# Second expert layer wholly in high and low parts, with the expert blocks' work on the other engines put in another order

## The reference, cut to what matters

```
z      = layer_norm(x)                      # 4096 tokens x 256
assign = argmax(z @ centroids.T)            # one of 8 experts for each token
xn     = layer_norm(z) * ln_g[e] + ln_b[e]
h      = relu(xn @ w1[e].T + b1[e])         # first layer:  256 -> 1024
y      = z + h @ w2[e].T + b2[e]            # second layer: 1024 -> 256
out    = x + sigmoid(z . centroid[e]) * y + (1 - sigmoid(..)) * z
```

## Time and profile before

| what | value |
|---|---|
| time, median of 3 runs | 1053.16 us (1052.61 to 1053.6) |
| the profiled execution's own time | 1052.73 us |
| its span | 1050.9 us |
| PE busy | 1041.6 us (99%) |
| DVE, ACT, POOL busy | 844.9, 688.7, 565.3 us |
| expert blocks on TensorE | from about 799.6 us to the end |

### The profile page before, as it was taken

One profiled execution on the slowest core, in us unless ns is written; L12 is line 12 of the kernel. 1 busy time (PEld: TensorE's weight loads), 2 busy tenths in 40 slices (PEclk: granted clock), 3 DMA queues, 4 the chain that ended last, 5 costly groups with the idle time before them and its releaser, 6 DMA issues.

```text
span 1050.9 us, 24670 instructions
## 1 busy us (share of the span) xinstructions
PE 1041.6 (99%) x8610; PEld 940.5 (89%) x8610; DVE 844.9 (80%) x1979; ACT 688.7 (66%) x1838; POOL 565.3 (54%) x665
## 2 busy tenths in 40 slices
PE   9999999999999999999999999999999999999997
PEld 7889898988888888889898989889888999999997
DVE  7878888878888888888888879888887797767663
ACT  6765757675666767666757575766566666676761
POOL 1744464646454555545464646465444667566663
PEclk9999999999999999999999999999999999999999
DMA  6665657585757576767667585856356868777760
GB/s 212 160 169 148 170 156 189 146 215 142 201 146 197 142 193 155 200 156 197 159 168 185 142 210 137 213 144 171 91 153 196 307 198 294 250 234 234 249 194 31
DMA packets 159666, 190.57 MB, mean 181 GB/s; under 512 B 17454, under 2 KB 149038, under 8 KB 154673
## 3 DMA queue, kind: packets, MB, share of 16 engines
q1 hardware_dynamic: 155088, 179.09, 62.4%
q0 software_dynamic: 3360, 8.53, 2.2%
q10 hardware_dynamic: 1088, 1.31, 0.4%
HBM read 65.72 MB, written 46.07 MB: 106 GB/s over the span
## 4 chain that ended last, share of the span: by engine, by line
PE 96%; DVE 2%; POOL 1%; ACT 1%; DMA 0%; issue 0%; POOLq 0%; DVEq 0%
PE psum L742 17%; PE psum L775 16%; PE psum L812 11%; PE psum L902 10%; PE psum L791 10%; PE psum L827 9%; PE psum L761 8%; PE psum L938 6%; PE psum L932 5%; PE psum L830 1%; PE psum L883 1%; PE psum L914 1%; DVE neg_max L1410 1%; DMA c_in<-in_ctx_in 0%; PE psum L856 0%; DVE w_lo L1545 0%
## 5 line engine op out<-in xcount | busy, mean ns | idle before, releaser
L1823 POOL TENSOR_TENSOR prob<-prob,inv_sum 128x512 f32<-128x512 f32 x172 | 177.7, 1047 | 190.1 <-DVE inv_sum L1416 189.2
L1133 ACT ACTIVATE prob<-psum,neg_max 128x256 f32<-128x256 f32 x344 | 160.2, 478 | 38.8 <-DVE neg_max L1410 38.5
L1410 DVE TENSOR_REDUCE neg_max<-psum 128x2 f32<-128x512 f32 x256 | 161.9, 672 | 27.7 <-PE psum L791 27.5
L1422 DVE STREAM_TRANSPOSE prob<-prob 128x512 f32<-128x512 f32 x172 | 118.5, 698 | 12.3 <-POOL prob L1823 11.9
L1823 POOL TENSOR_TENSOR w_ring<-w_ring,inv_sum 128x512 f32<-128x512 f32 x76 | 78.1, 1041 | 76.0 <-DVE inv_sum L1416 75.7
L1140 ACT ACTIVATE head_out_hi<-psum 128x512 fp32r<-128x512 f32 x52 | 31.1, 597 | 105.6 <-PE psum L812 102.4
L1119 ACT ACTIVATE v_n<-psum 128x512 f32<-128x512 f32 x128 | 77.9, 608 | 26.7 <-PE psum L775 22.7
L1108 ACT ACTIVATE k_hi<-psum 128x512 fp32r<-128x512 f32 x128 | 77.0, 603 | 22.0 <-PE psum L742 21.3
L1461 DVE TENSOR_TENSOR k_lo<-psum,k_hi 128x512 fp32r<-128x512 f32 x128 | 85.7, 674 | 0.0
L742 PE MATMUL psum<-kv_t_hi,w_hi 128*128 128x512 f32 x252 | 85.0, 419 | 0.0
L775 PE MATMUL psum<-w_hi,kv_t_hi 128*128 128x512 f32 x256 | 80.2, 395 | 0.4 <-DVE k_lo L1461 0.4
(11 more groups left out here) (215 smaller groups left out, 2952.4 us busy)
## 6 DMA issues: line engine op xcount, KB each, us to landing
sorted_rows<-filler SPq DMA_DIRECT2D x54, 660.0 KB
prob_t<-prob SPq DMA_DIRECT2D x172, 128.0 KB, 2.8
w_ring<-prob SPq DMA_DIRECT2D x172, 128.0 KB, 2.7
w<-in_experts SPq DMA_DIRECT2D x19, 1024.0 KB, 7.8
w_ring<-in_experts SPq DMA_DIRECT2D x18, 1024.0 KB, 6.7
prob_t<-w_ring SPq DMA_DIRECT2D x76, 128.0 KB, 2.8
w_ring<-w_ring SPq DMA_DIRECT2D x76, 128.0 KB, 2.7
w_ring<-normed SPq DMA_DIRECT2D x56, 128.0 KB, 3.0
```

The source lines that it names most:

```text
L1133: act.activation(prob_at(u, bb)[:, :, parity, i], scores_i, ACT.Exp, bias=neg_max[:, at, i:i + 1], accum_out=prob_sum[:, at, i:i + 1]).the ...
L1410: dve.tensor_reduce(neg_max[:, (4 * u + n) % 8, :], psum[:, n, :].rearrange("p (i j) -> p i j", i=2), AXIS_X, ALU.max, negate=True).then_i ...
L1422: dve.transpose(probs, probs).then_inc(s_quad, 1)
L1823: pool.tensor_tensor(probs, probs, inverse, ALU.mult).then_inc(s_soft, 1)
```

## The change

The second layer of the blocks from slot 1 on is made wholly in parts: all four hidden pieces are split, all 2048 elements of the second weights are split, and the float32 products are gone. The hidden pieces pass through two places (`hid_raw[:, piece % 2]`), so relu of a piece waits for the split of the piece two before. Products of the low weights come last of the three passes, with the wait for them just ahead. On ScalarE and VectorE the first weights are split three blocks ahead instead of two, `high_weights_2` stays last on ScalarE, and VectorE does `low_weights_1` between the two halves of `finish`. The second weights' buffer is free again when its low part is made, not when the products have run.

```
 def load_weights_2(s):
-    if s >= NW2:
-        wait_made(sp, ("fy", s - NW2, 1))
+    if s == NW2:
+        wait_made(sp, ("fy", 0, 1))
+    elif s > NW2:
+        sp.wait_ge(f_w2l, s - NW2 - FIRST_SPLIT + 1)

 def layer_2_split(s):                                   # TensorE
+    pe.wait_ge(f_w2h, s - FIRST_SPLIT + 1)
+    pe.wait_ge(f_hl, FC // 2 * (s - FIRST_SPLIT + 1))
+    def products(bank, i, n): ...                       # 8 products of pass n
     for i in range(2):
         bank = begin(("fy", s, i))[:, 0:d_model]
-        # in_parts: 3 passes x 4; plain: 4 float32 products
+        products(bank, i, 0)
+        products(bank, i, 1)
+        if i == 0:
+            pe.wait_ge(f_w2l, s - FIRST_SPLIT + 1)
+        products(bank, i, 2).then_inc(f_y, 1)

 def relu_parts(s):                                      # ScalarE
     for i in range(FC // 2):
         act.wait_ge(f_h, FC // 2 * (s - 1) + i + 1)
-        if i < FS // 2 and s > FIRST_SPLIT:
-            act.wait_ge(f_hl, FS // 2 * (s - 1 - FIRST_SPLIT) + i + 1)
-        elif i == FS // 2 and s >= 2:
-            wait_made(act, ("fy", s - 2, 1))
+        piece = FC // 2 * (s - FIRST_SPLIT) + i
+        if piece >= 2:
+            act.wait_ge(f_hl, piece - 1)

 # ScalarE, loop
-for s in range(n_early, n_slots):
-    run(s + 2, (normalise_rows,), (high_weights_1,))
+for s in range(n_early - 1, n_slots):
     run(s + 1, (relu_parts,))
     run(s + 2, (row_gain_bias,))
+    run(s + 3, (normalise_rows,), (high_weights_1,))
     run(s + 1, (high_weights_2,))

 # VectorE: ahead of late_blocks and in the loop
+low_weights_1(5)
 late_blocks()
 finish(2)
-for s in range(n_early, n_slots):
-    run(s + 2, (low_weights_1,))
+for s in range(n_early - 1, n_slots):
     run(s + 1, (split_hidden,))                         # 4 pieces, was 2
     run(s + 2, (split_xn,))
     run(s + 3, (transpose_rows,))
-    run(s, (finish,))
+    run(s, (finish_half, 0))
+    run(s + 3, (low_weights_1,))
+    run(s, (finish_half, 1))

 def high_weights_2(s), low_weights_2(s):                # ScalarE, GpSimd
-    w2_ring[s % NW2][:, 0:FS * d_model]                 # 1024 elements
+    w2_ring[s % NW2][:]                                 # 2048 elements
```

More of the change, by code:

```diff
@@ L320, in build @@
             hid_raw = y_t[:].rearrange("p c b t -> p c (b t)")
[L321 to L322 removed]
+            w2_hl = [[w[:].rearrange(rule)[:, 0:n_w].rearrange("p (f d) -> p f d", f=FC) for w in pair] for pair, rule in
                      ((head_out, "p b c t -> p (b c t)"), (w_o, "p c n -> p (c n)"))]
@@ L919, in layer_2_split @@
                 def layer_2_split(s):
[L921 to L933, removed]
-                        return last
@@ L936, in plain @@
[L936 to L943, removed]
@@ L955, in layer_2_split, with products @@
-                    bank = begin(("fy", s, 1))[:, 0:d_model]
-                    plain(bank, 1, True)
-                    in_parts(bank, 1, False).then_inc(f_y, 1)
+                    pe.wait_ge(f_w2h, s - FIRST_SPLIT + 1)
+                    pe.wait_ge(f_hl, FC // 2 * (s - FIRST_SPLIT + 1))
+                    def products(bank, i, n):
+                        hw, hx = PASSES[n]
+                        for f in range(FC):
+                            last = pe.matmul(bank, hid_hl[hx][:, s % 2, f, i * P:(i + 1) * P], w2_hl[s % 2][hw][:, f, :],
+                                             start=(n == 0 and f == 0), stop=(n == 2 and f == FC - 1))
+                        return last
@@ new lines, in layer_2_split @@
+                    if s == FIRST_SPLIT:
+                        banks = [begin(("fy", s, i))[:, 0:d_model] for i in range(2)]
+                        for i in range(2):
+                            products(banks[i], i, 0)
+                            products(banks[i], i, 1)
+                        pe.wait_ge(f_w2l, 1)
+                        for i in range(2):
+                            products(banks[i], i, 2).then_inc(f_y, 1)
+                        return
+                    for i in range(2):
+                        bank = begin(("fy", s, i))[:, 0:d_model]
+                        products(bank, i, 0)
[3 more added lines that the diff above has]
+                        products(bank, i, 2).then_inc(f_y, 1)
@@ L1636, in low_weights_1, with split_hidden @@
                                       ALU.subtract).then_inc(f_wl, 1)
-                def split_hidden(s):
-                    for i in range(FS // 2):
+                def split_hidden(s, pieces=range(FC // 2)):
+                    for i in pieces:
                         dve.wait_ge(f_ha, FC // 2 * (s - 1) + i + 1)
@@ new lines, in split_hidden, with finish_half @@
+                        raw = hid_raw[:, (FC // 2 * (s - FIRST_SPLIT) + i) % 2, :]
+                        then_next(dve.tensor_copy(hi, raw))
+                        dve.tensor_tensor(lo, raw, hi, ALU.subtract).then_inc(f_hl, 1)
+                def finish_half(i, s):
+                    if i == 0:
+                        dve.wait_ge(f_b[s % NR], 16 * (s // NR + 1))
+                        if s == 0:
+                            dve.wait_ge(s_nrm, n_pairs)
+                        else:
+                            dve.wait_ge(f_o, 2 * s)
+                    item = ("fy", s, i)
+                    wait_made(dve, item)
+                    if i == 0 and s >= 2:
+                        dve.wait_ge(f_out[s % 2], 32 * (s // 2))
+                    last_reads(item, dve.tensor_tensor(fin[:, s % 2, i, :], work_bank(number[item])[:, 0:d_model],
+                                                      b2_ring[:, s % NR, :], ALU.add))
+                    if i == 0:
+                        dve.wait_ge(f_base, s + 1)
+                    wait_read(dve, item)
+                    dve.scalar_tensor_tensor(out=fin[:, s % 2, i, :], in0=fin[:, s % 2, i, :],
+                                             scalar=rows_at(s)[:, i, COL_ALPHA:COL_ALPHA + 1],
+                                             in1=base[:, s % NR, i, :], op0=ALU.mult, op1=ALU.add).then_inc(f_o, 1)
```

77 lines of the change are left out of this document (26 added, 51 removed).

## The result

The changed kernel takes 1108.66 us (median of 5 runs, 1107.83 to 1109.44) against 1053.47 beside it: a ratio of 1.0524, 95% interval 1.0509 to 1.0539. It is slower by 55 us; the forecast was 1107. The profiled execution has a span of 1106.2 us, against 1050.9 before.

The account below looks back on a forecast made before the run. VectorE, held by GpSimd's long subtraction, was to bound the kernel at 9.87 + 4.1 + 0.86 = 14.8 us a block; 16.7 (block 4) + 35.1 + 2 = 54 us on 1052.73 gives 1107 us, range 1072 to 1138.

Parts of the forecast that it names:

- the hold: Each block: GpSimd's 4.59 us subtraction keeps VectorE out of SBUF, except beside line 1658 (0.46); costs VectorE 4.1 us.
- TensorE, 11.50 a block: TensorE's products per block: 8 float32 products (3.46 us) go, 24 in parts (2.87) come; 11.50 us, 0.59 less.
- VectorE's 9.87: VectorE's own work per block with two more hidden pieces split: 9.87 us, under 11.50 if nothing holds it up.
- the rival of a shorter hold: Rival, chance 0.08: a long subtraction lets VectorE in after 2.4 us, costing 1.9; period 12.6, time 1074 us.
- Slips of 0.86: GpSimd's base operations and scatters slip in ahead of VectorE's subtractions: 0.43 us a block seen, taken twice as 0.86.
- the 14.4 worked out from it: Alternative period by the Trainium skill: only GpSimd's base operations slip in, not its scatters; nearer 14.4 us than 14.8.
- The first blocks, 16.7: Up to block 4: VectorE's added work delays plan, weight loads and block 4's end by 16.7 us; range 10.1 to 22.
- The sign that I named: Sign of being right: TensorE gap of 8 us or more at block 4 or 5, behind ScalarE's wait for slot 6's weights.
- 35.1 and 2: Later blocks: blocks 5 to 17 lose 13 x 2.7 = 35.1 us, block 18 some 2 more.
- The clock: Rival, chance 0.03: TensorE, waiting 3 us a block, drops to 1.2 GHz; 23.0 us a block, 1213 us.
- TensorE stays the bound: Rival, chance 0.07: GpSimd's subtraction falls beside VectorE work it does not hold up; period 11.50, time 1042 us.
- rival 1054.5: Rival, chance 0.05: no port conflict, but block 4 is 10.1 us late and 14 blocks return 8.3; 1054.5, no change.

Follow-up runs that it names:

- e1: The changed kernel with GpSimd's subtraction for the low second weights cut to 64 of 2048 elements, the other low parts not made; 1053.51 us, ratio 1.0001.
- e2: The changed kernel with GpSimd's subtraction for the low second weights cut to 1024 of 2048 elements, the other low parts not made; 1068.61 us, ratio 1.0146.
- e3: The changed kernel with the whole subtraction for the low second weights done by VectorE instead of GpSimd; 1076.84 us, ratio 1.0219.
- e8: The kernel before with only GpSimd's subtraction doubled to 2048 elements, the upper half writing low parts that no product reads; 1070.29 us, ratio 1.0159.
- e10: The changed kernel with ScalarE's high second weights of block 4 moved back ahead of block 6's normalising and high first weights; 1106.56 us, ratio 1.0509.
- e5: The kernel before with only the new order on ScalarE and VectorE, half of the second layer staying in float32; 1063.24 us, ratio 1.0098.

## Why the prediction was right

The time was predicted to 2 us, and its main reason, the hold, is shown by e1, e2 and e3. That the sum came so close is luck: the first blocks cost 7.1 us more than forecast, and all behind them 5.6 us less.

- **TensorE, 11.50 a block.** Right: 11.52 in e1, where nothing else is in the way.
- **VectorE's 9.87 and the hold of 4.1.** Right. The hold measures 3.89 (4.38 - 0.49) and scales with the subtraction (e2). One of 4.6 us holds to its end, so the rival of a shorter hold falls: it had 1074, and its 1.9 us are near what the 1024 elements of e2 cost (2.18 - 0.49 = 1.69).
- **Slips of 0.86.** Half: only two subtractions are stretched (0.92 and 0.85 for 0.69, as in the earlier trace rows), 0.4 us. The double that I took for work that loses its idle time did not come, and the period was 14.40 instead of 14.8. The two stand beside the base operations (1004.28 to 1006.14); the subtractions beside the scatters keep their 0.69. That is what a sentence of the Trainium skill ("SBUF — State Buffer", section "Who interferes with whom") made of it, and the 14.4 worked out from it beside the forecast was the better number, in part by chance: the hold was 0.2 us shorter than forecast, and 0.2 us of waiting for ScalarE, which the forecast put at nothing, made up for it. For the other direction the rows contradict it: a scatter beside VectorE's low first weights takes 3.13 us (e8, 961.61), and 1.05 to 1.19 beside short ones.
- **The first blocks, 16.7.** Too small; 23.8 measured, above even the upper end of 22. The chain was the right one, in its order: plan, SyncE's queue, ScalarE's wait for block 6's weights, block 4's second weights, GpSimd, TensorE. The plan came at 878.38, not 874.7: VectorE also waited twice for 1.87 us on ScalarE (the row at 864.38 and one at 847.19), which I had only in the upper bound. The step to ScalarE took 7.2 us instead of 6.65, and the last 32 products 5.6 instead of 3.84, at a granted clock of 0.88 (895.0 to 909.5). By the runs, 8.1 us come without a long subtraction (e1), 5.7 with 1024 elements (e2) and 10.0 with the second 1024, near e8's 9.0, of which 2.6 are slow products. The sign that I named, a gap of 8 us or more on TensorE at block 4 or 5, did not come: its longest wait there is 4.36 us (ahead of 886.54), and the lateness adds up over four blocks. With ScalarE's queue out of the way (e10) 20.4 of the 23.8 remain, so with that chain shortened another ends only 3.4 us earlier.
- **Blocks 6 to 18.** 35.1 and 2 were predicted, 37.1 together, from a period 0.4 too long; 28.4 (12 of the 13 periods) and 3.1 (the last one and the end) came, 31.5 together.
- **The clock.** The granted clock is 0.87, 0.89 and 0.88 in three windows of the first blocks (835 to 850, 880 to 895, 895 to 909.5), a mean between its lower level (0.5, 1.2 GHz) and its upper one (1.00, 2.4 GHz), where TensorE had waits of some us. The Trainium skill ("TensorE: Matmul & The Clock Gate", Part 1) has that tendency right. The rival's 1213 did not come: in the window 996.2 to 1010.6 the clock is 1.00 in the changed kernel and 0.88 in e10, and the period is 14.40 in both. The wait covers it, as the forecast had it for that case; only the products of block 4 paid, some 1.8 us. In e8 and e5, where TensorE leads at that point, nothing covers it: the products behind its waits of 4.92 and 6.45 us took some 2.6 and 2 us longer. Nor was it right that no stretch of the trace before shows a lower clock: from 1043.0 to 1050.8, with TensorE busy for 2.20 us, it is 0.84.
- **TensorE stays the bound.** Wrong with GpSimd's subtraction, and instructive: e1 shows that even without it the chain of the first blocks takes all of the gain (rival 1054.5; measured 1053.5). One argument for it was misread: line 1663 is held in two later blocks of the kernel before, at 905.03 (1.89 us, a sixth case beside the five counted) and at 1024.37 (1.63).

## What to carry to other kernels

Count a long GpSimd instruction on SBUF operands as time of VectorE, at GpSimd's duration, unless it stands beside idle time or instructions that it does not hold; if VectorE's own price for that work is lower, do it there. A stage with slack takes such an instruction for nothing (e8's later blocks), a stage without it pays (e8's first blocks), and how much depends on which instruction is caught, so look at each stage. When an order is moved further ahead, follow what now queues behind the first item whose data are not there yet, and check whether the gain per block repays the one-time loss.

## What was not expected of the hardware

- GpSimd's drain ahead of its first conditional block is 5.84 to 9.33 us long in the changed kernel and the runs, and ends 1.85 or 2.21 us after the landing of the scatter issued just before it. In e8, where it is 9.33, 7.50 us of delay reached TensorE.
- A start together of the two engines (852.17 and 852.18) went one after the other, VectorE first: 2.28, and GpSimd's 6.74 in place of 4.6. At 835.73 and 835.75 it was VectorE, recorded 0.02 us earlier, that was held (4.65). What decides is open.
